# Routed experts: turning the gated product inside the next up product, and down one step behind up

## What is computed

```
scores = softmax(xt @ Wg.T)                      # 16 experts in 4 groups, top 2 groups, top 4 experts
h = silu(einsum('td,eid->eti', xt, W1)) * einsum('td,eid->eti', xt, W3)
expert_out = einsum('eti,edi->etd', h, W2)
y = einsum('etd,te->td', expert_out, combine)
z = silu(xt @ Ws1.T) * (xt @ Ws3.T) @ Ws2.T      # shared expert
out = x + y + z
```

## Time and profile before

| | us |
|---|---|
| median of 3 runs | 397.82 (397.6 to 398.34) |
| the profiled execution | 396.75 |
| its span, first to last instruction | 395.0 |
| attention stage | 0 to 133 |
| shared expert and routing | 133 to 198.8 |
| routed tiles | 198.8 to 387 |
| last additions and output | 387 to 395.0 |

### The profile page before, as it was taken

How to read it: one execution, slowest core, us unless ns; L and a number is a source line. 1 busy time by engine, 2 the same in 40 slices (tenths; PEclk the granted TensorE clock), 3 DMA queues, 4 the chain that set the end, 5 groups by cost and what they waited for, 6 DMA issues and landing times.

```text
span 395.0 us, 8998 instructions
## 1 busy us (share of the span) xinstructions
PE 385.2 (98%) x2146; PEld 280.1 (71%) x2147; DVE 244.3 (62%) x676; ACT 162.8 (41%) x494; POOL 178.6 (45%) x225
## 2 busy tenths in 40 slices
PE   7999999999999999999999999999999999999996
PEld 6788888888888646555667675446777777777765
DVE  3577577987988465788735434444445554646465
ACT  5347656564564463101124333333333333334431
POOL 3164323337888574565553333333333333334334
PEclk9999999999999999999999999999999999999999
DMA  7974574358878996256267973334374637363748
GB/s 255 367 245 138 161 280 145 133 201 284 305 255 318 416 420 273 92 208 225 92 197 243 322 238 114 102 116 135 122 250 138 237 116 242 114 231 109 267 112 302
DMA packets 37812, 84.14 MB, mean 213 GB/s; under 512 B 5680, under 2 KB 25616, under 8 KB 35728
## 3 DMA queue, kind: packets, MB, share of 16 engines
q1 hardware_dynamic: 31248, 64.83, 49.3%
q0 software_dynamic: 6528, 18.88, 12.2%
HBM read 60.21 MB, written 23.48 MB: 212 GB/s over the span
## 4 chain that ended last, share of the span: by engine, by line
PE 78%; DVE 11%; DMA 4%; issue 2%; ACT 2%; POOL 0%; DVEq 0%; SPq 0%; POOLq 0%; ACTq 0%
PE heads L1381 18%; PE bank L1455 13%; PE heads L1270 11%; PE heads L1423 7%; PE heads L1272 5%; PE bank L1436 5%; PE bank L1402 4%; PE heads L1391 4%; DVE kv L733 3%; PE bank L1284 3%; PE heads L1373 3%; DMA y_scratch<-toep,dest_i 2%; PE bank L1447 2%; DVE prod L762 2%; DMA xn_tr_all<-y_scratch 2%
## 5 line engine op out<-in xcount | busy, mean ns | idle before, releaser
L716 POOL DMA_INDIRECT y_scratch<-toep,dest_i x72 | 70.2, 975 | 112.9 <-DVE dest_i L1130 95.2
L1381 PE MATMUL heads<-experts,toep 128*128 x256 | 86.5, 461 | 0.6 <-DVE toep L1088 0.5
L1270 PE MATMUL heads<-toep,kv 128*128 128x256 f32 x256 | 77.9, 386 | 1.9 <-DVE kv L733 1.3
L661 POOL DMA_INDIRECT rows_scratch<-rows,slot_i x64 | 63.2, 988 | 35.6 <-issue 19.6
L1455 PE MATMUL bank<-experts,toep 88*128 x256 | 66.1, 381 | 1.2 <-DVE toep L1095 1.2
L553 ACT ACTIVATE toep<-heads 128x176 f32<-128x176 f32 x72 | 22.8, 317 | 77.9 <-PE heads L1381 68.1
L1381 PEld LDWEIGHTS heads<-experts,toep 128*128 128x128 f32 x256 | 43.7, 190 | 14.7 <-issue 1.1
L1272 PEld LDWEIGHTS heads<-toep,kv 128*128 128x128 f32 x256 | 48.7, 190 | 6.5
L762 DVE TENSOR_TENSOR prod<-heads,ctx_rep 128x1024 f32<-128x1024 f32 x32 | 39.1, 1221 | 22.3 <-PE bank L1284 19.9
L1095 DVE COPY toep<-heads 88x256 f32<-88x256 f32 x72 | 30.2, 420 | 31.8 <-PE heads L1391 31.5
L1272 PE MATMUL heads<-toep,kv 128*128 128x128 f32 x256 | 49.2, 274 | 0.0
(11 more groups left out here) (240 smaller groups left out, 500.0 us busy)
## 6 DMA issues: line engine op xcount, KB each, us to landing
ctx_rep<-ctxr_in SPq DMA_DIRECT2D x16, 1024.0 KB, 5.0
experts<-experts_in SPq DMA_DIRECT2D x16, 608.0 KB, 15.4
toep<-rows_scratch SPq DMA_DIRECT2D x56, 144.0 KB
prod<-y_scratch SPq DMA_DIRECT2D x5, 1024.0 KB, 5.6
rows_scratch<-pad_row SPq DMA_DIRECT2D x17, 144.0 KB, 1.8
ctx_tr<-ctxt_in SPq DMA_DIRECT2D x16, 128.0 KB, 5.1
toep<-toep_in SPq DMA_DIRECT2D x4, 512.0 KB, 6.9
ctx_n<-ctx_in SPq DMA_DIRECT2D x16, 128.0 KB, 2.0
```

The costliest lines, as they stand in the source:

```text
L661: pool.indirect_dma_start(rows_d, bass.IndirectOffsetOnAxis(ap=slot_i[:, u, k:k + 1].bitcast(U32), axis=0), rows[:, u, :], None).then_inc( ...
L716: pool.indirect_dma_start(y_d, bass.IndirectOffsetOnAxis(ap=dest_i[b][:, 0:1].bitcast(U32), axis=0), y_sb[b], None).then_inc(y_sent[b], 16)
L1270: nc.tensor.matmul(y_ps[par][:, i, :], kv[:, q, 0, h * P:(h + 1) * P], toep[:, q * HH + h, :], start=True, stop=False)
L1381: last = nc.tensor.matmul(up_ps[p], x_tr[p][:, blk, :], up_w(e, blk), start=blk == 0, stop=blk == LB - 1)
```

## The change

On PE, `turn_h(t - 1)` moves from the end of step t into `up(t)`, between the matmuls of block 0 and those of block 1, and the last piece of the step becomes `down(t - 1)` instead of `down(t - 2)`. After the loop one `down` is left instead of two. On DVE `copy_h(t - 1)` now stands ahead of `hidden(t)` instead of behind it. On ACT `store_y(t - 1)` takes the place of `store_y(t - 2)`. No instruction is added or removed.

```
@@ scalar engine
-                if not (isinstance(t, int) and t < 2):
-                    store_y(t - 2, p, (b - 2) % DEPTH, before if b >= 2 else before - 1)
+                if not (isinstance(t, int) and t == 0):
+                    store_y(t - 1, 1 - p, (b - 1) % DEPTH, before if b >= 1 else before - 1)
...
@@ vector engine
                 take(t, b, before)
+                if not (isinstance(t, int) and t == 0):
+                    copy_h(t - 1, 1 - b % 2)
                 hidden(t, b % 2, b)
                 if isinstance(t, int) and t < 2:
                     add_z(UNITS - 2 + t)
-                if not (isinstance(t, int) and t == 0):
-                    copy_h(t - 1, 1 - b % 2)
                 place(t, b, before)
@@ tensor engine, up (the mixed form has the same two lines)
                 for blk in range(LB):
+                    if blk == 1 and not (isinstance(t, int) and t == 0):
+                        turn_h(t - 1, 1 - p)
                     last = nc.tensor.matmul(up_ps[p], x_tr[p][:, blk, :],
@@ tensor engine, routed_step
-                elif not (isinstance(t, int) and t == 1):
-                    if isinstance(t, int) and t < 4:
-                        pe.wait_ge(z_added, UNITS - 3 + t)
-                    down(t - 2, p, (b - 2) % DEPTH)
-                if not (isinstance(t, int) and t == 0):
-                    turn_h(t - 1, 1 - p)
+                else:
+                    if isinstance(t, int) and t < 3:
+                        pe.wait_ge(z_added, UNITS - 2 + t)
+                    down(t - 1, 1 - p, (b - 1) % DEPTH)
...
             turn_h(LIVE - 1, (LIVE - 1) % 2)
-            for t in range(LIVE - 2, LIVE):
-                down(t, t % 2, t % DEPTH)
+            down(LIVE - 1, (LIVE - 1) % 2, (LIVE - 1) % DEPTH)
```

More of the change, by code:

```diff
@@ L594, in routed_step @@
                     src_tr(t + 1, 1 - p)
-                if not (isinstance(t, int) and t < 2):
-                    store_y(t - 2, p, (b - 2) % DEPTH, before if b >= 2 else before - 1)
+                if not (isinstance(t, int) and t == 0):
+                    store_y(t - 1, 1 - p, (b - 1) % DEPTH, before if b >= 1 else before - 1)
             routed(act, routed_step, 2 * DEPTH)
-            for t in range(LIVE - 2, LIVE):
-                store_y(t, t % 2, t % DEPTH, t // DEPTH)
+            store_y(LIVE - 1, (LIVE - 1) % 2, (LIVE - 1) % DEPTH, (LIVE - 1) // DEPTH)
             for i in range(2):
@@ L1372, in up @@
                     for blk in range(LB):
+                        if blk == 1:
+                            turn_h(t - 1, 1 - p)
                         nc.tensor.matmul(up_ps[p][0:HALF], x_tr[p][:, blk, 0:HALF],
```

## The result

| | before | after |
|---|---|---|
| median, us | 397.71 (397.58 to 398.34) | 413.27 (412.82 to 413.71) |
| ratio, 95% interval | | 1.0386 (1.0367 to 1.0405) |
| span of the profiled execution, us | 395.0 | 411.6 |
| forecast | | 409.3, range 405 to 415 |

The direction and the range held; the size was 4 us short. Of all runs in this document one, the longest of e8_before_unrolled (407.92 us), was in a slower state of the chip; it stands in the median given there and not in the ratio.

A forecast was written before the change was run, and what follows sets the result against it. PE was taken as the bound, busy 98% of the span, so the change could only move waits. Terms 9.9 + 2.6 - 1.3 + 0.6 - 0.2 = +11.6, say 11.5, on 397.8 gave 409.3 us, range 405 to 415.

The forecast's parts named there:

- `down`'s wait, 58 x 0.17: In 58 ordinary steps `down`'s weight load waits 0.17 us for `copy_h`: +9.9 us.
- The way before, "some 3.5 us": Before the change, some 3.5 us of other PE work was said to lie between `turn_h` and its `down`.
- `src_tr`, no cost on top: `up`'s wait for ACT's copy: slack 0.04 to 0.10, cost 0; 0.07 to 0.13 if `down` were not late.
- `hid` for `turn_h`, no cost: `turn_h` inside `up` finds the product of `hidden` ready: slack 0.54 us, cost 0.
- Steps 1, 3, 5: +0.3, +1.5, +0.8: Early steps: step 1 longer, `down` held behind DVE's small arithmetic (`last_needs`, `last_counts`) in the others; +0.3, +1.5, +0.8 us.
- What comes back, -1.3: `y` stored one step sooner, so `place` finds its send landed and two waits of `down` go: -1.3 us.
- Mixed tiles, +0.6: Mixed steps 16 to 23: 36 changes between halves and whole array against 32, +0.6 us.
- The end, -0.2, and the end passes to PE: After the last `up`: -0.2 us in all; the earlier send of tile 67 gains 0, since PE sets the end.
- rival three: Both waits bite: the next `up` also waits, for `src_tr` or the expert's register load; 415.3 us, chance 0.13.

The follow-up runs named there:

- e8_before_unrolled: The kernel before with PE's loop of routed steps 28 to 59 written out; 403.79 us, ratio 1.0137.
- e5: The kernel after with one more DVE copy, of 92 columns into unused space, ahead of each `copy_h`; 423.33 us, ratio 1.0646.
- e3: The kernel after with the two turned blocks of `hid` in separate banks, each copied and waited for by itself; 405.58 us, ratio 1.0199.
- e12: The kernel after with e3 and e4 together, and ACT's copy of the turned rows split the same way; 399.51 us, ratio 1.0041.
- e6: The kernel before with the same added DVE copy as e5, ahead of each `copy_h`; 399.24 us, ratio 1.0028.
- e4: The kernel after with the register load of the next tile's expert moved ahead of `down`'s wait, loop kept; 408.27 us, ratio 1.0257.
- e11: e12 with DVE's thirteen small operations one behind each of steps 2 to 14 instead of in two blocks; 397.71 us, ratio 1.0006.
- e2: The kernel before with `turn_h` moved inside `up` and `copy_h` ahead of `hidden`, `down` and store still two steps behind; 404.28 us, ratio 1.0158.
- e9: e2 with the next expert's register load moved ahead of `down`, as in e4; 404.45 us, ratio 1.0167.

## Why the prediction was right, and where it was short

- **`down`'s wait, 58 x 0.17.** Right: load 1.09 behind `turn_h`, hole 0.17, steps of 2.66. e5 shows the cause by its dose, e3 and e12 by taking it away.
- **The way before, "some 3.5 us".** Wrong, as is "a whole `down`" in the section on the change; the sum was worked out from the new order and does not suffer. No `down` stood between `turn_h` and the `down` that uses it: from the transposes at 302.02 one `up` and one `turn_x` lead to its weight load at 303.54, shown above. That is 1.52, of which 1.09 was needed. The slack was 0.43; the change shortens the way by one block of `up`, 0.60, and 0.17 is missing. The expectation of e6 took the 1.5 for slack in the same way.
- **`src_tr`, no cost on top.** Right, and so was its role as the next in line: 0.12 in e3, forecast 0.07 to 0.13. e12, with all three waits relieved, is back at 2.49.
- **`hid` for `turn_h`, no cost.** Right.
- **Steps 1, 3, 5: +0.3, +1.5, +0.8.** The intervals from `turn_x` of 1, 4 and 6 grew by 0.23, 1.38 and 0.59. 2.2 instead of 2.6.
- **What comes back, -1.3.** Nearly right. The three long steps of before, 2.98, 3.19 and 2.81 (from 5, 11 and 36), are 2.65, 2.93 and 3.09. That of 5 is gone; that of 11 is not quite, since the send still holds `place` for 0.44; that of 36 is now the first step of a loop turn, and is 2.66 in e4, where the turns cost nothing. About 1.2 came back.
- **Mixed tiles, +0.6.** From `turn_x` of 15 to that of 27: 34.61 before, 35.21 in e12, where no wait is left. +0.60. In after, with three or four ordinary waits in this stretch, 35.85.
- **The end, -0.2, and the end passes to PE.** From the last `turn_x` to the end of the span 14.4 before and 14.3 after. The last pieces of the chain after are PE's unit sums and ACT's copy of unit 14, and DVE starts its last addition ahead of that copy, at 407.47:

```profile
402.33 1.13 PE bank L1458 x4
...
406.05 1.74 PE bank L1521 x8
407.79 0.02 issue
407.81 0.38 ACT resid L602
```
```profile
407.47 0.42 DVE L1206 TENSOR_TENSOR resid<-resid,xn_tr_all 128x256 f32<-128x256 f32 x1
```

- **The step that fell short** is the term that was not in the sum: the register load at the turns of PE's loop. It stood under rival three ("the load of the expert's number, which now stands behind a `down` that has been held up, is no longer hidden"), priced at 0.1 in 60 steps, with a chance of 0.13. In the written-out steps the load is indeed hidden, by less than 0.1 us. At a turn the jump stands in front of it. The rows of before held the warning: 0.06 to spare at each turn, and a `turn_h` behind `down` that the change takes away. The first step of a turn takes about 0.44 more than 2.66, and the other three some 0.15 together. From step 28 to 60 this adds up to 4.8 us, of which 0.5 belongs to the four steps at turns of DVE's loop, long in e4 too. So 4.3 are the register load's. By medians it is 5.0 (413.27 to 408.27 in e4).

The forecast made 9.9 + 2.6 - 1.3 + 0.6 = 11.8 us of the routed stage, and the table adds up to 16.4. The difference is 4.3 for the register load, 0.5 for DVE's loop, which the forecast did not look at, 0.1 for what did not come back, less 0.4 for the early steps; 0.1 belongs to no one place. The medians are 15.6 apart; the spans, 16.6, are of one execution each.

Where the 15.4 us (3.86%) of the change go, by ratios, with 1 to 2 us of uncertainty in each difference: 5.1 to the register load (e4), 8.6 more to the waits for the two copies (e4 to e12), 1.4 to the blocks of small arithmetic (e12 to e11). What is left in e11, 0.2, is below what is measured, but it is a balance and not the absence of costs. By the profiles the 71 distances of e11 add up to 2.9 us more than before: 1.2 in the step of 6, 1.9 in four steps of DVE's loop, 0.6 in the mixed tiles, 0.3 in steps 1 and 2, less 1.3 that came back. Against that, the way from the last `turn_x` to the end is 12.8 us long instead of 14.4 (12.9 in e12, but 14.3 in after). So the order does have something to give, some 3 us at three long steps and, with the copies split, at the end. In the ordinary steps it gives nothing: the kernel before kept PE full there with nobody waiting, and a `down` closer to its `up` shortens no chain that sets the time.

The Trainium skill has a figure for such a load (DMA: Bandwidth & Descriptors, the table on latency and other measured facts): a floor of about 600 ns, and loops unrolled four times to spread it. The traces here show 0.30 us for the instruction and 0.67 until the weight load that uses the register, close to that figure. The loop of four steps a turn does not hide it here, since each step has a load of its own; e4 hides it by issuing it ahead of the wait.

## What to carry to other kernels

A wait of PE is priced by two numbers, not one: how late the data is, and what the sequencer may no longer do in advance because it stands at the wait. So before moving a consumer closer to its producer, list the register loads and the loop jump that follow the wait, see how much they have to spare at a turn and not only in an ordinary step, and put the loads ahead of the wait; one moved instruction was worth 4 to 5 us here. And count the way from producer to consumer in starts: "two steps behind" was 1.52 us here, with a slack of 0.43. Where an engine is full, taking more than the slack only uncovers the copy: 0.42 us, with 0.41 from the first transpose to its start and 0.26 behind its end.

## What the runs showed of the hardware that was not expected

- From the start of a register load to the weight load that uses it: 0.67 to 0.69 us, in three places where nothing else held it, for an instruction of 0.30 to 0.36.
- A register load behind the jump of PE's loop started 0.67 to 0.74 ahead of its use in the kernel before, and 1.0 to 1.2 ahead in most other ordinary steps.
- Two DVE copies in a row start 0.17 apart where the first has 92 columns and a bar of 0.25 (e5). Two of 128 columns start 0.20 to 0.21 apart with bars of 0.28. A bar overstates what an operation costs its queue.
- Writing out PE's loop of 32 steps made the kernel before slower by 1.4% (e8). In the one run that was profiled, transfers landed late; why is open.
- PE goes on 0.24 after ACT's copy in written-out steps and 0.14 in its loop (e2, e9). One sequencer instruction more in the written-out steps would fit.
